# The attention sums as split float32r products in place of full fp32 products

## The chip, the core and the metric

The kernel runs on one core of a Trainium2 chip. The metric is device time in microseconds (us), the median of several executions; lower is better. Engines are named as in the profile: PE (TensorE matmuls), PEld (TensorE's loads of stationary weights, which overlap matmuls), DVE (VectorE), ACT (ScalarE), POOL (GpSimd) and SP (which issues the transfers).

## The reference

Input X has 4 batches of 512 rows with 512 features. For each batch the reference computes a modulated layer norm, an attention block whose "attention" is one vector per batch, and a feed-forward block:

```
Xn = layernorm(h); Q, K, V = split(Xn @ W_in + b_in)
K = rotary(K); V = rotary(V)                 # first 256 features
A = sum over rows of cos_sim(K) * cos_sim(V) # one vector of 512 per batch
A = 0.5 * A + 0.5
Y = (A * Q) @ W_out + b_out
...
out = x + gb * (relu(h2 @ W_up.T) @ W_down.T + h2 @ W_expert)
```

The change concerns the sum over rows that makes A, a vector with one number for each of the 512 features of a batch.

## The kernel before

Most products are done with operands split in a high and a low part of type float32r, `x = hi + lo`, and three matmuls (hi·hi, hi·lo, lo·hi); the helper `three` (lines 1032 to 1036) issues them, so that nearly all matmuls carry the lines 1034 to 1036. The tiles are 128 partitions wide; a batch has 4 row tiles (t) and 4 feature chunks (c or k).

The kernel has an order written out by hand for each engine, and semaphores between engines. For each batch b, `attention(b)` on PE does: the K and V tile of rows 0 (`kv_tile`), the output projection of the batch before (`out_rows_of(b - 1)`, which reads `g_hi` and `g_lo`), K and V of rows 1 to 3, four Q chunks (`feature_chunk`) with the transposes of the next batch between them, and last `a_sums(b)`. Then comes `kv_tile(b + 1, 0)`; behind batch 3 the feed-forward part begins with the logits (lines 1161 and 1162).

`acc`, 128 partitions by 768, gathers on DVE the weighted products of K and V over the four row tiles (`kv_sum`). After the last of them `a_pairs` (lines 734 to 737) folds the rotary part into `pair`, and `a_sums` adds over the 128 partitions: four full fp32 matmuls with 128x128 weights out of `pair` and `acc` and a one-column operand out of `half` (0.5 or 1). They write 4 columns of PSUM bank 6. That bank is also the one in which chunk 2 of the next batch's transposes stands until `t_split(b + 1, 2)` (line 688) on DVE has read it, and so `a_sums` waits for `afold` (the folding) and for the third `t_los` (that split).

Behind `a_sums`, DVE turns the sums into `a_col` and `ab_col` (`a_evac`, lines 741 and 744), ACT scales Q with them and rounds it to `g_hi` (lines 507 and 510), and DVE makes `g_lo` (`q_split`, line 748). `out_rows_of(b)` waits for these chunk by chunk.

POOL waits for the third `afold` of each batch (line 405) and then does, without another wait in batches 1 and 2, four `base` additions (line 356, both inputs in SBUF) and in batch 3 four `low_part` subtractions (line 330). In batch 0 it waits for `wlo_out` too, which DVE gives later.

`split_v` (lines 907 to 911) at the start of the kernel is a place where DVE does the same pair of operations as the change adds: a rounding copy of 128x512 and a subtraction of 128x512, all in SBUF.

Of the kernel before, what the change touches and what calls it, by code (L numbers as in the profile page):

```python
# [4 lines left out]
P = 128  # L5
B, S, D = 4, 512, 512
NT = S // P
NC = D // P
ROT = D // 4
# [4 lines left out]
IDENTITY_WEIGHT = 0.5  # L14
# [17 lines left out]
SUM_BANK = 6  # L32
# [3 lines left out]
def build(nc, X, cols, ident, rot, w, wmod, brow, out):  # L36
    f32 = mybir.dt.float32
    f32r = mybir.dt.float32r
    ALU = mybir.AluOpType
# [11 lines left out]
    with ctx:  # L51
        def sb(name, shape, dt=f32):
            return ctx.enter_context(nc.sbuf_tensor(name, shape, dt))

        def sem(name):
            return ctx.enter_context(nc.semaphore(name))
# [10 lines left out]
        g_hi = sb("g_hi", [P, NC, S], f32r)  # L67
        g_lo = sb("g_lo", [P, NC, S], f32r)
# [13 lines left out]
        acc = sb("acc", [P, D + 2 * ROT])  # L82
# [3 lines left out]
        gate_abs = hb[0:B, 1, 2:4]  # L86
        col = sb("col", [P, COLS])
        idn = sb("idn", [P, P])
        half = sb("half", [P, 2])
        xnm = sb("xnm", [P, NT])  # L90
        fold = cross[:].rearrange("p (i r) -> p i r", i=2)
        pair = sb("pair", [P, 2, ROT])
        ones = pair[0:1, 0, :]
        expo = sb("expo", [P, NT])
        sc = sb("sc", [P, NC * B])
        sc_t = sb("sc_t", [P, 3, NC * B])
# [19 lines left out]
        a_col = sb("a_col", [P, NC])  # L116
# [7 lines left out]
        tsum = sb("tsum", [P, NT])  # L124
# [3 lines left out]
        ps = ctx.enter_context(nc.psum_tensor("ps", [P, 8, 512], f32))  # L128
# [14 lines left out]
        cst = sem("cst")  # L143
# [16 lines left out]
        lg_ps2 = sem("lg_ps2")  # L160
        bc_ps = sem("bc_ps")
        afold = sem("afold")
        xst_s, xmv_s, xve_s, xrs_s = (sem(n) for n in ("xst_s", "xmv_s", "xve_s", "xrs_s"))
        xnm_s = sem("xnm_s")
        xn_s = sem("xn_s")
# [12 lines left out]
        a_ps, a_sb, ab_sb = sem("a_ps"), sem("a_sb"), sem("ab_sb")  # L178
# [134 lines left out]
        def _(pool):  # L313
# [3 lines left out]
            def rstd_x(g):  # L317
                pool.wait_ge(xve_s, g + 1)
                power(xrs[:], xve[:], NT, xrs_s)
# [94 lines left out]
                else:  # L414
                    low_part(5, whi, (3,) * NC, wlo_expert)

            pool.wait_ge(cst, 4)
            rstd_x(0)
            rstd_h(0, 0, 2)
            rstd_h(0, 2, 2)  # L420
# [185 lines left out]
        def _(dve):  # L606
            v = nc.vector
# [13 lines left out]
            def x_stats(g):  # L621
                dve.wait_ge(x_in, g * 16 + 16)
                for t in range(NT):
                    v.bn_stats(xst[:, t, :], xs[:, tok(g, t)]).then_inc(xst_s, 1)

            def x_aggr(g):
                for t in range(NT):
                    dve.wait_ge(xst_s, g * NT + t + 1)
                    v.bn_aggr(xmv[:, t, :], xst[:, t, :]).then_inc(xmv_s, 1)
                dve.wait_ge(xmv_s, g * NT + NT)  # L630
                v.tensor_scalar(xve[:], xmv[:, :, 1], EPS, None, ALU.add).then_inc(xve_s, 1)
# [97 lines left out]
            def a_pairs(b):  # L729


                dve.wait_ge(kacc, b * NT + NT)
                blocks = acc[:].rearrange("p (g i r) -> p g i r", g=3, i=2)
                v.tensor_tensor(fold, blocks[:, 0:3:2, 0, :], blocks[:, 0:3:2, 1, :], ALU.add).then_inc(afold, 1)
                dve.wait_ge(afold, b * 3 + 1)
                v.tensor_tensor(pair[:, 0, :], fold[:, 0, :], fold[:, 1, :], ALU.add).then_inc(afold, 1)
                v.tensor_tensor(pair[:, 1, :], fold[:, 0, :], fold[:, 1, :], ALU.subtract).then_inc(afold, 1)

            def a_evac(b):
                dve.wait_ge(a_ps, b + 1)  # L740
                v.tensor_scalar(a_col[:], ps[:, SUM_BANK, 0:NC], 1.0 - IDENTITY_WEIGHT, IDENTITY_WEIGHT,
                                ALU.mult, ALU.add).then_inc(a_sb, 1)
                dve.wait_ge(a_sb, b + 1)
                v.tensor_tensor(ab_col[:], a_col[:], col[:, COL_BQ:COL_BQ + NC], ALU.mult).then_inc(ab_sb, 1)

            def q_split(b, c):
                dve.wait_ge(q_his, b * NC + c + 1)
                v.tensor_tensor(g_lo[:, c, :], ps[:, Q_BANKS[c], :], g_hi[:, c, :].bitcast(f32),  # L748
                                ALU.subtract).then_inc(q_los, 1)
# [17 lines left out]
            def finish_rows(b):  # L767
                o_evac(b, 0)
                o_evac(b, 1)
                x2_out(b, 0)  # L770
                o_evac(b, 2)
                x2_out(b, 1)
                o_evac(b, 3)

            def attention(b):
                if b > 0:
                    a_evac(b - 1)
                    for c in range(NC):
                        q_split(b - 1, c)
                if b == 0:  # L780
                    x_stats(1)
                    x_aggr(1)
                    dve.wait_ge(const_in, N_CONST)
                    dve.wait_ge(row_out, 32)
                kv_rows(b, 0)
                if b == 0:
                    x_shift(1)
                kv_products(b, 0)
                if b > 0:
                    finish_rows(b - 1)  # L790
                    if b + 2 < B:
                        x_mean(b + 2)
                kv_sum(b, 0)
                if 0 < b < B - 1:
                    h_row(b + 1, 0)
                    h_row(b + 1, 1)
                    h_stats(b + 1, 0)
                    h_stats(b + 1, 1)
                    h_aggr(b + 1, 0, 2)
                elif b == B - 1:  # L800
                    for t in range(NT):
                        x2_rows(B, t)
                    h_aggr(B, 0, NT)
                kv_rows(b, 1)
                if b > 0 and b + 2 < B:
                    x_var(b + 2)
                kv_products(b, 1)
                if 0 < b < B - 1:
                    h_shift(b + 1, 0, 2)
                    h_row(b + 1, 2)  # L810
                    h_row(b + 1, 3)
                    h_stats(b + 1, 2)
                    h_stats(b + 1, 3)
                elif b == 0:
                    h_row(1, 0)
                    h_row(1, 1)
                    h_stats(1, 0)
                    h_stats(1, 1)
                    h_aggr(1, 0, 2)
                else:  # L820
                    h_shift(B, 0, NT)
                kv_sum(b, 1)
                kv_rows(b, 2)
                if 0 < b < B - 1:
                    h_aggr(b + 1, 2, 2)
                elif b == 0:
                    h_shift(1, 0, 2)
                    h_row(1, 2)
                    h_row(1, 3)
                    h_stats(1, 2)  # L830
                    h_stats(1, 3)
                    h_aggr(1, 2, 2)
                    x_mean(2)
                kv_products(b, 2)
                if b < B - 1:
                    h_shift(b + 1, 2, 2)
                if b + 2 < B and b > 0:
                    x_shift(b + 2)
                kv_sum(b, 2)
                kv_rows(b, 3)  # L840
                kv_products(b, 3)
                t_split(b + 1, 0)
                t_split(b + 1, 1)
                kv_sum(b, 3)
                a_pairs(b)
                if b == 0:
                    x_var(2)
                t_split(b + 1, 2)
                t_split(b + 1, 3)
                if b == 0:  # L850
                    x_shift(2)
                    for k in range(NC):
                        split_lo_out(k)

            v.memset(half[:, 0:1], 1.0).then_inc(cst, 1)
            v.memset(half[:, 1:2], 0.5).then_inc(cst, 1)
            v.memset(ones, 1.0).then_inc(cst, 1)
            v.memset(expo[:], -0.5).then_inc(cst, 1)
            dve.wait_ge(c_exp, 1)
            v.tensor_scalar(sc_t[:, 1, :], sc_t[:, 0, :], 1.0, None, ALU.add).then_inc(c_steps, 1)  # L860
            dve.wait_ge(c_steps, 1)
# [130 lines left out]
            def ffn(b):  # L992
# [23 lines left out]
                else:  # L1016
                    for i in range(len(LAST_PARTS)):
                        d_evac_last(i)

            a_evac(B - 1)  # L1020
            for c in range(NC):
                q_split(B - 1, c)
# [6 lines left out]
        def _(pe):  # L1029
            mm = nc.tensor.matmul  # L1030
# [54 lines left out]

            def a_sums(b):

                pe.wait_ge(afold, b * 3 + 3)
                pe.wait_ge(t_los, (b + 1) * NC + 3)
                a = ps[:, SUM_BANK, :]  # L1090
                mm(a[:, 0:1], pair[:, 0, :], half[:, 1:2], start=True, stop=True)
                mm(a[:, 1:2], pair[:, 1, :], half[:, 1:2], start=True, stop=True)
                mm(a[:, 2:3], acc[:, 2 * P:3 * P], half[:, 0:1], start=True, stop=True)
                mm(a[:, 3:4], acc[:, 3 * P:4 * P], half[:, 0:1], start=True, stop=True).then_inc(a_ps, 1)

            def out_rows_of(b):
                for t in range(NT):
# [161 lines left out]
```

## Time and profile before

| what | us |
|---|---|
| median of 3 executions (389.91 to 392.1) | 390.7 |
| the profiled execution: its own time | 388.38 |
| the profiled execution: span from first to last instruction | 386.6 |
| PE busy | 365.2 |
| DVE busy | 254.0 |
| ACT busy | 167.3 |
| POOL busy | 112.4 |

The span is shorter than the execution's own time by 1.8 us, which lie ahead of the first and behind the last instruction. The busy time of PE counts matmuls that overlap in the pipeline and is no measure of how well it is used.

### The profile page before, as it was taken

The page shows a single profiled execution, that of the slowest core. Times are in us where ns is not written, and L with a number is a line of the kernel's source. Part 1 is how long each engine was busy: PE and PEld are TensorE (multiplying, and loading weights), DVE is VectorE, ACT ScalarE, POOL GpSimd, SP SyncE. Part 2 cuts the span into 40 slices and gives each one's busy share as a digit, 9 for nine tenths or more (in the row PEclk, how much of TensorE's full clock was granted, in tenths as well). Part 3 has the DMA queues.
Part 4 walks back from the last instruction along what each step waited for, and adds up shares of the span by engine and source line. Part 5 has one row for each costly group of instructions (what it writes and reads, how often), then busy time and mean ns, then how long its engine had stood idle before and what let it go on. Part 6 is the DMA issues. An engine that isn't in the chain of part 4 may idle for free.

```text
span 386.6 us, 4661 instructions
## 1 busy us (share of the span) xinstructions
PE 365.2 (94%) x1664; PEld 286.1 (74%) x1664; DVE 254.0 (66%) x519; ACT 167.3 (43%) x293; POOL 112.4 (29%) x112
## 2 busy tenths in 40 slices
PE   4897998799989999999999999989999999999996
PEld 0156886687867778888788878868788878887885
DVE  0679799569978679886887556746560755084354
ACT  1337386685336830366215772147113612551210
POOL 0115683247842518425162151910001001000000
PEclk9997999899999999999999999999999999999999
DMA  7997972041001000000000003000200110011002
GB/s 226 384 376 253 362 255 89 0 137 27 2 20 63 0 0 2 27 2 2 0 29 0 0 2 108 28 2 27 81 2 0 54 57 0 0 57 54 2 0 109
DMA packets 10950, 27.42 MB, mean 71 GB/s; under 512 B 1184, under 2 KB 1568, under 8 KB 9776
## 3 DMA queue, kind: packets, MB, share of 16 engines
q1 hardware_dynamic: 10928, 27.13, 19.9%
q8 instruction: 13, 0.21, 0.2%
q14 instruction: 9, 0.07, 0.1%
HBM read 22.90 MB, written 4.23 MB: 70 GB/s over the span
## 4 chain that ended last, share of the span: by engine, by line
PE 72%; DVE 9%; ACT 5%; DMA 4%; issue 4%; POOL 4%; SPq 1%; POOLq 0%; DVEq 0%; ACTq 0%
PE ps L1034 21%; PE ps L1036 20%; PE ps L1035 20%; PE ps L1058 3%; PE ps L1041 3%; DMA xs<-in_wmod 2%; DMA xs<-in_X 2%; ACT sqj L448 1%; PE ps L1161 1%; PE ps L1162 1%; PE ps L1049 1%; DVE hb L662 1%; DVE ps L695 1%; POOL xs L350 1%; DVE acc L726 1%
## 5 line engine op out<-in xcount | busy, mean ns | idle before, releaser
L1034 PE MATMUL ps<-w_hi,t_hi 128*128 128x512 f32 x192 | 75.9, 396 | 1.3 <-DVE prod L707 1.3
L1035 PE MATMUL ps<-w_lo,t_hi 128*128 128x512 f32 x192 | 75.2, 392 | 0.0
L1036 PE MATMUL ps<-w_hi,t_lo 128*128 128x512 f32 x192 | 75.2, 392 | 0.0
L1034 PE MATMUL ps<-w_hi,g_hi 128*128 128x512 f32 (+1 forms) x132 | 51.5, 390 | 0.5 <-DVE g_lo L748 0.5
L1034 PE MATMUL ps<-t_hi,w_hi 128*128 128x512 f32 x128 | 51.8, 405 | 0.0
L1036 PE MATMUL ps<-w_hi,g_lo 128*128 128x512 f32 (+1 forms) x132 | 50.6, 383 | 0.0
L1035 PE MATMUL ps<-w_lo,g_hi 128*128 128x512 f32 (+1 forms) x132 | 50.6, 383 | 0.0
L1036 PE MATMUL ps<-t_hi,w_lo 128*128 128x512 f32 x128 | 50.5, 394 | 0.0
L1035 PE MATMUL ps<-t_lo,w_hi 128*128 128x512 f32 x128 | 50.5, 394 | 0.0
L688 DVE TENSOR_TENSOR t_lo<-ps,t_hi 128x512 fp32r<-128x512 f32 x32 | 21.8, 687 | 36.2 <-ACT t_hi L499 36.0
L1034 PEld LDWEIGHTS ps<-w_hi,t_hi 128*128 128x128 f32 x192 | 36.5, 190 | 9.2 <-issue 1.7
L1036 PEld LDWEIGHTS ps<-w_hi,t_lo 128*128 128x128 f32 x192 | 36.4, 190 | 7.7
L1035 PEld LDWEIGHTS ps<-w_lo,t_hi 128*128 128x128 f32 x192 | 36.5, 190 | 7.5
L324 POOL TENSOR_TENSOR hrs<-hve,expo 128x2 f32<-128x2 f32 (+1 forms) x12 | 10.7, 892 | 86.7 <-DVE hve L679 78.3
L448 ACT ACTIVATE sqj<-ps 128x512 bf16<-128x512 f32 x16 | 9.6, 597 | 56.7 <-DVE ps L695 43.4
L1034 PEld LDWEIGHTS ps<-w_hi,g_hi 128*128 128x128 f32 x132 | 24.8, 188 | 6.7 <-DVE g_lo L748 2.2
L1036 PEld LDWEIGHTS ps<-w_hi,g_lo 128*128 128x128 f32 x132 | 24.8, 188 | 4.9
L1036 PEld LDWEIGHTS ps<-t_hi,w_lo 128*128 128x128 f32 x128 | 24.4, 191 | 5.4
L1034 PEld LDWEIGHTS ps<-t_hi,w_hi 128*128 128x128 f32 x128 | 24.5, 191 | 5.2
L1035 PEld LDWEIGHTS ps<-w_lo,g_hi 128*128 128x128 f32 x132 | 24.8, 188 | 4.6
L1035 PEld LDWEIGHTS ps<-t_lo,w_hi 128*128 128x128 f32 x128 | 24.5, 191 | 4.9
L1058 PE MATMUL ps<-idn,z 128*128 128x128 f32 x128 | 18.6, 286 | 9.6 <-ACT z L485 4.9
(130 smaller groups left out, 601.0 us busy)
## 6 DMA issues: line engine op xcount, KB each, us to landing
xs<-in_X SPq DMA_DIRECT2D x4, 1024.0 KB, 7.2
stage<-in_w SPq DMA_DIRECT2D x4, 1024.0 KB, 6.9
out<-xs SPq DMA_DIRECT2D x15, 256.0 KB, 2.0
xs<-in_wmod SPq DMA_DIRECT2D x3, 1024.0 KB, 10.6
xs<-in_wmod SPq DMA_DIRECT2D x8, 256.0 KB, 7.0
stage<-in_w SPq DMA_DIRECT2D x8, 256.0 KB, 9.5
gate_bc<-mod_rows SPq DMA_DIRECT2D x8, 256.0 KB, 6.9
gate_bc<-in_wmod SPq DMA_DIRECT2D x1, 1024.0 KB, 12.6
```

The costliest lines, as they stand in the source:

```text
L324: nc.gpsimd.tensor_tensor(hrs[:, t0:t0 + n], hve[:, t0:t0 + n], expo[:, 0:n], ALU.pow).then_inc(hrs_s, n)
L350: nc.gpsimd.tensor_tensor(xs[:, tok(b, t)], xs[:, tok(b, t)], h, ALU.add).then_inc(x2_pool, 1)
L448: nc.scalar.activation(sqj[:], src, ACT.Square, accum_out=nsq[:, t % 2, i:i + 1]).then_inc(nsq_s, 1)
L662: v.tensor_tensor(h, h, sa_bc[:], ALU.add).then_inc(h1_s, 1)
L688: v.tensor_tensor(t_lo[:, g % 2, c, :], ps[:, T_BANKS[c % 2], :], t_hi[:, g % 2, c, :].bitcast(f32), ALU.subtract).then_inc(t_los, 1)
L695: v.tensor_tensor(ps[:, k_bank, :], ps[:, k_bank, :], bkv_bc[:, 0, :], ALU.add).then_inc(kb_s, 1)
L726: v.scalar_tensor_tensor(acc[:], prod[:], wgt[:, t % 2:t % 2 + 1], acc[:], ALU.mult, ALU.add).then_inc(kacc, 1)
L1034: mm(dst, l_hi, r_hi, start=start, stop=False)
L1035: mm(dst, l_hi, r_lo, start=False, stop=False)
L1036: return mm(dst, l_lo, r_hi, start=False, stop=stop)
L1041: last = mm(ps[0:B, bank, :], sc[:, k * B:(k + 1) * B], src[:, k * D:(k + 1) * D], start=(k == 0), stop=(k == NC - 1))
L1058: last = nc.tensor.transpose(ps[:, T_BANKS[c % 2], t * P:(t + 1) * P], z[:, t, c * P:(c + 1) * P], idn[:])
```

## The change

The folded sums go back into the first 256 columns of `acc` rather than into `pair`. A new function `a_split` on DVE rounds the 512 columns of `acc` to float32r in chunk 0 of `g_hi` and puts the remainder in chunk 0 of `g_lo`; both chunks are free at that place, between the output projection of the batch before and the Q chunks of this batch. `a_sums` then waits for `asplit` and issues eight float32r matmuls (a high and a low one for each of 4 chunks) with both columns of `half`; each chunk has two result columns, one with weight 1 and one with 0.5, and `a_evac` picks one of them in two instructions instead of one. At the start `half` is made by a copy, since it is float32r now.

```diff
+        half = sb("half", [P, 2], f32r)
+        sums_hi = g_hi[:, 0, :]
+        sums_lo = g_lo[:, 0, :]
...
-            pool.wait_ge(cst, 4)
+            pool.wait_ge(cst, 5)
...
-                v.tensor_tensor(pair[:, 0, :], fold[:, 0, :], fold[:, 1, :], ALU.add).then_inc(afold, 1)
-                v.tensor_tensor(pair[:, 1, :], fold[:, 0, :], fold[:, 1, :], ALU.subtract).then_inc(afold, 1)
+                v.tensor_tensor(acc[:, 0:ROT], fold[:, 0, :], fold[:, 1, :], ALU.add).then_inc(afold, 1)
+                v.tensor_tensor(acc[:, ROT:2 * ROT], fold[:, 0, :], fold[:, 1, :], ALU.subtract).then_inc(afold, 1)
+
+            def a_split(b):
+
+                dve.wait_ge(afold, b * 3 + 3)
+                v.tensor_copy(sums_hi, acc[:, 0:D]).then_inc(asplit, 1)
+                dve.wait_ge(asplit, b * 2 + 1)
+                v.tensor_tensor(sums_lo, acc[:, 0:D], sums_hi.bitcast(f32), ALU.subtract).then_inc(asplit, 1)
 
             def a_evac(b):
                 dve.wait_ge(a_ps, b + 1)
-                v.tensor_scalar(a_col[:], ps[:, SUM_BANK, 0:NC], 1.0 - IDENTITY_WEIGHT, IDENTITY_WEIGHT,
+                v.tensor_scalar(a_col[:, 0:2], ps[:, SUM_BANK, 1:4:2], 1.0 - IDENTITY_WEIGHT, IDENTITY_WEIGHT,
                                 ALU.mult, ALU.add).then_inc(a_sb, 1)
-                dve.wait_ge(a_sb, b + 1)
+                v.tensor_scalar(a_col[:, 2:4], ps[:, SUM_BANK, 4:8:2], 1.0 - IDENTITY_WEIGHT, IDENTITY_WEIGHT,
+                                ALU.mult, ALU.add).then_inc(a_sb, 1)
+                dve.wait_ge(a_sb, b * 2 + 2)
...
                 a_pairs(b)
+                a_split(b)
                 if b == 0:
                     x_var(2)
                 t_split(b + 1, 2)
...
+            dve.wait_ge(cst, 2)
+            v.tensor_copy(half[:], tsum[:, 0:2]).then_inc(cst, 1)
...
             def a_sums(b):
 
-                pe.wait_ge(afold, b * 3 + 3)
+                pe.wait_ge(asplit, b * 2 + 2)
                 pe.wait_ge(t_los, (b + 1) * NC + 3)
                 a = ps[:, SUM_BANK, :]
-                mm(a[:, 0:1], pair[:, 0, :], half[:, 1:2], start=True, stop=True)
-                mm(a[:, 1:2], pair[:, 1, :], half[:, 1:2], start=True, stop=True)
-                mm(a[:, 2:3], acc[:, 2 * P:3 * P], half[:, 0:1], start=True, stop=True)
-                mm(a[:, 3:4], acc[:, 3 * P:4 * P], half[:, 0:1], start=True, stop=True).then_inc(a_ps, 1)
+                for j in range(NC):
+                    mm(a[:, 2 * j:2 * j + 2], sums_hi[:, j * P:(j + 1) * P], half[:], start=True, stop=False)
+                    done = mm(a[:, 2 * j:2 * j + 2], sums_lo[:, j * P:(j + 1) * P], half[:], start=False, stop=True)
+                done.then_inc(a_ps, 1)
```

On DVE, at the end of batch 1 and in the order in which the engine takes them, the kernel before has these instructions (`t_lo` x2 are `t_split` of chunks 2 and 3 of the next batch):

```order
L726 SCALAR_TENSOR_TENSOR acc<-prod,wgt,acc 128x768
L734 TENSOR_TENSOR cross<-acc 128x256
L736 TENSOR_TENSOR pair<-cross 128x128
L737 TENSOR_TENSOR pair<-cross 128x128
L688 TENSOR_TENSOR t_lo<-ps,t_hi 128x512 x2
L741 TENSOR_SCALAR a_col<-ps 128x4
L744 TENSOR_TENSOR ab_col<-a_col,col 128x4
```

The changed kernel has at the same place of DVE (its line numbers are some higher: `t_split` is L691, `a_split` L745 and L747):

```order
L729 SCALAR_TENSOR_TENSOR acc<-prod,wgt,acc 128x768
L737 TENSOR_TENSOR cross<-acc 128x256
L739 TENSOR_TENSOR acc<-cross 128x128
L740 TENSOR_TENSOR acc<-cross 128x128
L745 CAST g_hi<-acc 128x512
L747 TENSOR_TENSOR g_lo<-acc,g_hi 128x512
L691 TENSOR_TENSOR t_lo<-ps,t_hi 128x512 x2
L751 TENSOR_SCALAR a_col<-ps 128x2
L753 TENSOR_SCALAR a_col<-ps 128x2
L756 TENSOR_TENSOR ab_col<-a_col,col 128x4
```

Two instructions of 128x512 stand between the folding and the two splits of the transposes now, and `a_col` is made in two.

## Rows read from the trace of the kernel before

**Rows 1.** The page: busy time by engine, and the chain that ended last by engine.
```profile
PE 365.2 (94%) x1664; PEld 286.1 (74%) x1664; DVE 254.0 (66%) x519; ACT 167.3 (43%) x293; POOL 112.4 (29%) x112
...
PE 72%; DVE 9%; ACT 5%; DMA 4%; issue 4%; POOL 4%; SPq 1%; POOLq 0%; DVEq 0%; ACTq 0%
```

**Rows 2.** PE's waits, smallest groups: total us, times, longest.
```profile
PE ps L1058 <- issue: 1.6, 1, 1.6
...
PE ps L1034 <- DVE g_lo L748: 0.5, 2, 0.3
```

**Rows 3.** PEld's timeline at the end of batch 1: start us, us, instruction.
```profile
129.83 0.41 PEld L1091 LDWEIGHTS ps<-half,pair 128*128 128x128 f32 x2
...
130.83 0.19 PEld L1034 LDWEIGHTS ps<-w_hi,t_hi 128*128 128x128 f32 x1
130.94 0.19 PEld L1035 LDWEIGHTS ps<-w_lo,t_hi 128*128 128x128 f32 x1
```

**Rows 4.** DVE's timeline at the end of batch 1.
```profile
127.70 0.42 DVE L734 TENSOR_TENSOR cross<-acc 128x256 f32<-128x256 f32 x1
128.16 0.29 DVE L736 TENSOR_TENSOR pair<-cross 128x128 f32<-128x128 f32 x1
128.37 0.28 DVE L737 TENSOR_TENSOR pair<-cross 128x128 f32<-128x128 f32 x1
128.57 1.28 DVE L688 TENSOR_TENSOR t_lo<-ps,t_hi 128x512 fp32r<-128x512 f32 x2
...
131.23 1.30 DVE L744 TENSOR_TENSOR ab_col<-a_col,col 128x4 f32<-128x4 f32 x1
```

**Rows 5.** POOL's timeline behind the folding of batches 0, 1 and 3.
```profile
82.26 10.11 POOL L356 TENSOR_TENSOR hb<-hb,bo_bc 128x512 f32<-128x512 f32 x8 [4.85 <-DVE w_lo L618]
...
128.73 5.02 POOL L356 TENSOR_TENSOR hb<-hb,bo_bc 128x512 f32<-128x512 f32 x4 [3.97 <-DVE pair L737]
...
222.10 5.03 POOL L330 TENSOR_TENSOR w_lo<-stage,w_hi 128x512 fp32r<-128x512 f32 x4 [7.68 <-DVE pair L737]
```

**Rows 6.** DVE's timeline, split_v of chunks 1 and 3 of a weight.
```profile
33.02 0.89 DVE L909 CAST w_hi<-stage 128x512 fp32r<-128x512 f32 x1
33.94 1.64 DVE L911 TENSOR_TENSOR w_lo<-stage,w_hi 128x512 fp32r<-128x512 f32 x1
...
38.77 0.42 DVE L909 CAST w_hi<-stage 128x512 fp32r<-128x512 f32 x1
39.23 0.69 DVE L911 TENSOR_TENSOR w_lo<-stage,w_hi 128x512 fp32r<-128x512 f32 x1
```

**Rows 7.** POOL's timeline beside split_v of chunk 1.
```profile
31.92 1.71 POOL L330 TENSOR_TENSOR w_lo<-stage,w_hi 128x512 fp32r<-128x512 f32 x1 [0.51 <-ACT w_hi L454]
...
33.71 1.32 POOL L330 TENSOR_TENSOR w_lo<-stage,w_hi 128x512 fp32r<-128x512 f32 x1
```

**Rows 8.** DVE's last folding instruction of batches 2 and 3.
```profile
175.12 0.29 DVE L737 TENSOR_TENSOR pair<-cross 128x128 f32<-128x128 f32 x1
...
221.73 0.28 DVE L737 TENSOR_TENSOR pair<-cross 128x128 f32<-128x128 f32 x1
```

**Rows 9.** PEld's first load of a_sums in batches 2 and 3.
```profile
176.59 0.41 PEld L1091 LDWEIGHTS ps<-half,pair 128*128 128x128 f32 x2
...
223.19 0.41 PEld L1091 LDWEIGHTS ps<-half,pair 128*128 128x128 f32 x2
```

**Rows 10.** DVE's timeline at the end of batch 0; in brackets idle time and releaser.
```profile
77.58 0.69 DVE L688 TENSOR_TENSOR t_lo<-ps,t_hi 128x512 fp32r<-128x512 f32 x1 [1.27 <-ACT t_hi L499]
...
82.13 0.16 DVE L744 TENSOR_TENSOR ab_col<-a_col,col 128x4 f32<-128x4 f32 x1
```

**Rows 11.** PE's timeline in the output projection of batch 1, around its fourth chunk.
```profile
138.20 0.39 PE L1036 MATMUL ps<-w_hi,g_lo 128*128 128x512 f32 x1
...
138.94 0.39 PE L1035 MATMUL ps<-w_lo,g_hi 128*128 128x512 f32 x1
```

**Rows 12.** PE's groups by line: busy us, mean ns of one, idle before.
```profile
L1049 PE MATMUL ps<-sc,gate_bc 128*128 128x4 f32 x32 | 3.7, 253 | 0.0
```

More of the change, by code:

```diff
@@ L88, in build @@
         idn = sb("idn", [P, P])
-        half = sb("half", [P, 2])
+        half = sb("half", [P, 2], f32r)
         xnm = sb("xnm", [P, NT])
         fold = cross[:].rearrange("p (i r) -> p i r", i=2)
-        pair = sb("pair", [P, 2, ROT])
-        ones = pair[0:1, 0, :]
+        pair = sb("pair", [1, ROT])
+        ones = pair[0:1, :]
+        sums_hi = g_hi[:, 0, :]
+        sums_lo = g_lo[:, 0, :]
         expo = sb("expo", [P, NT])
@@ L162, in build @@
         afold = sem("afold")
+        asplit = sem("asplit")
         xst_s, xmv_s, xve_s, xrs_s = (sem(n) for n in ("xst_s", "xmv_s", "xve_s", "xrs_s"))
@@ L853, in attention @@
                         split_lo_out(k)
-            v.memset(half[:, 0:1], 1.0).then_inc(cst, 1)
-            v.memset(half[:, 1:2], 0.5).then_inc(cst, 1)
+            v.memset(tsum[:, 0:1], 1.0).then_inc(cst, 1)
+            v.memset(tsum[:, 1:2], 0.5).then_inc(cst, 1)
             v.memset(ones, 1.0).then_inc(cst, 1)
             v.memset(expo[:], -0.5).then_inc(cst, 1)
+            dve.wait_ge(cst, 2)
+            v.tensor_copy(half[:], tsum[:, 0:2]).then_inc(cst, 1)
             dve.wait_ge(c_exp, 1)
```

## The prediction

> **What bounds the kernel now.** I read the page first: PE is busy 94% of the span and holds 72% of the chain that ended last [rows 1]. So what counts is whether PE issues without a break. The list of PE's waits comes next: behind the first 80 us it waits only in small pieces, among them 0.5 us for `g_lo` in the output projection of batch 0 and 1.6 us once in the feed-forward part [rows 2]. Any time by which PE is held or freed near `a_sums` therefore passes to the end, unless a later wait takes it up. That 1.6 us wait takes nothing up: it stands behind activations that follow from PE's own U chunks, and moves with them.
>
> Then the place itself, at the end of batch 1. PEld starts the loads for the sums at 129.83 and those of the next K tile at 130.83 [rows 3]. The third `t_los`, for which `a_sums` waits, comes from the first of the two `t_split` at 128.57; at 0.69 for one (the duration of such a subtraction in rows 6) it ends near 129.26 [rows 4, 6]. So PE's slack there is 129.83 − 129.26 = 0.57 us.
>
> **The products.** Before, four full fp32 products make eight loads and eight matmul records. Their loads take 130.83 − 129.83 = 1.00 us: the first waits 0.22 for the running matmul, the other seven follow at 0.11 [rows 3]. After, eight float32r products make eight loads. The first float32r load behind them was followed by the next after 130.94 − 130.83 = 0.11 us [rows 3], the same pace. Two products that add into the same few columns back to back have a row too: 32 records of 128x4 took 3.7 us, 0.115 each, in groups of four that accumulate [rows 12]. So I put the products at no change. Bounds: if they fell to nothing, 1.00 − 0.22 = 0.78 us a batch would be freed (3.1 us in all); if each cost the 0.25 that one record lasts instead of 0.115 [rows 12], 8 × 0.135 = 1.1 us a batch would be added (4.3 us).
>
> **The two DVE instructions without POOL.** The rounding copy takes 0.42 and the subtraction 0.69 where nothing disturbs them [rows 6]. A dependent DVE instruction starts 0.04 after the one before has ended (127.70 + 0.42 = 128.12, next at 128.16), and an independent one some 0.08 before that end (128.37 + 0.28 = 128.65, next at 128.57) [rows 4]. In batch 1 the folding ends at 128.37 + 0.28 = 128.65, the copy runs 128.69 to 129.11, the subtraction 129.15 to 129.84, and the `t_split` that PE needs runs from 129.76 to 130.45, 1.2 us later than now. With 0.05 to reach PE, an estimate near DVE's own 0.04, the loads start at 130.50, 0.67 late. Of this 0.11 comes back, since after a wait the second load follows 0.11 and not 0.22 behind the first. That is 0.56 us in batch 1, and the same sum gives 0.56 in batch 2 (folding ends 175.41, loads at 176.59) and in batch 3 (222.01 and 223.19) [rows 8, 9]. In batch 0 DVE sits idle 1.27 us for ACT ahead of that `t_split` [rows 10]; 0.42 + 0.69 + 2 × 0.04 = 1.19 fits into it, so the cost is nothing; without that cover it would be the same 0.56.
>
> **The two DVE instructions with POOL.** In batches 1 and 3, POOL's four instructions start at 128.73 and 222.10, 0.08 and 0.09 after the folding has ended [rows 4, 5, 8], just where `a_split` now begins; batch 2 has the same order of work. They have SBUF inputs and last 5.02 / 4 = 1.25 each. What such neighbours do to this very pair of DVE instructions is shown by `split_v`: beside POOL the copy took 0.89 instead of 0.42 and the subtraction 1.64 instead of 0.69 [rows 6]. The copy ended 0.28 after POOL's instruction had ended (31.92 + 1.71 = 33.63, copy 33.91). POOL's next ended at 33.71 + 1.32 = 35.03, some 1.12 after that copy, and the subtraction 0.55 later, at 35.58 [rows 6, 7]. So they took turns. Nearer by is `ab_col`, 128x4, which took 1.30 beside `base` [rows 4] and 0.16 where POOL was idle [rows 10]. The `t_split`, with one input in PSUM, kept its 1.28 for two while POOL ran from 128.73 on [rows 4, 5], so only the two new ones are hit. The Trainium skill, SBUF — State Buffer, Who interferes with whom, speaks against the change here: a VectorE instruction with two SBUF inputs contends with a GpSimd one that reads SBUF, the pair of ports goes whole to whoever starts first, and the other stands still until the end. By that rule alone the copy, if it starts first, goes free and the subtraction waits out one POOL instruction, which is the sum below; the rows above bear it out.
>
> In batch 1 the copy is due at 128.69 and POOL at 128.73, so I let DVE win: copy to 129.11, POOL's first then to 129.11 + 1.12 = 130.23, the subtraction to 130.78, `t_split` to 131.39, PE's loads at 131.44: 1.61 late, 1.50 net of the 0.11. Batch 2: folding ends 175.41, loads at 178.20 instead of 176.59: 1.50. Batch 3: 222.01, 224.80 instead of 223.19: 1.50. Sum 4.5 us.
>
> **What comes back.** Behind the sums, `ab_col` is stuck behind POOL now: 131.23 to 132.53. After the change POOL runs 0.4 to 1 us later and `ab_col` comes some 1.8 us later, behind a second `a_col` (0.1 us); it then ends about 0.9 to 1.1 us later than now, while PE is 1.5 later. In batch 1 PE waits shortly for the last `g_lo`: two matmuls on it stands at 138.94 instead of 138.20 + 2 × 0.23 = 138.66 (0.23 is the step left of the 1.00 above when seven of 0.11 go off), so 0.28 is lost there [rows 11] and comes back. Batch 2 has the same order of work, and I take the same. So −0.6 us in all. Batch 3 has the logits and two expert tiles ahead of its projection, and none.
>
> **The rest.** In batch 0 `ab_col` would move by 0.07 to 82.20, and POOL's eight additions start at 82.26 [rows 5, 10]. I let `ab_col` win and take nothing, since ACT normalises four tiles of batch 2 there before it can use it; if it lost, it would wait 1.25 and delay Q's chain, and PE which already waits for it [rows 2], by about 1.0. The small copy for `half` and POOL's fifth `cst` lie under the first loads, tens of us before anybody needs them: nothing, and with no cover 0.2. `base` and `low_part` end about 1 us later: `base` is read a whole batch later, and `wlo_expert` by an expert tile that moves 1.5 us itself.
>
> **Sum.** 4.5 − 0.6 = +3.9 us on the profiled execution, 388.38 to 392.3. That execution lies 2.3 under the median of the three; the step added to the median 390.7 gives 394.6, 1.0% slower.
>
> **The rivals.**
> *POOL first.* The order at the folding's end hangs on 0.04 us. If POOL takes the ports first, the copy waits until 128.73 + 1.25 + 0.28 = 130.26, POOL's second instruction runs to 131.38, the subtraction to 131.93 and the `t_split` to 132.54; PE is 2.76 late, 2.65 net. Three batches less 0.6: +7.4, 398.1. For it: `ab_col` loses every time POOL already runs. Against: DVE's own semaphore has reached it in 0.04, POOL in 0.08 [rows 4, 5].
> *No turns taken.* If the new pair is not held, the cost is 3 × 0.56 − 0.6 = +1.1, 391.8, which is no change to a measurement. Against: rows 6 and 7 show the same pair held.
> *The products get cheaper, and the kernel faster.* The place is PE between 129.83 and 130.83; the price is at most 0.78 us a batch. Over four batches it decides from 3.9 / 4 = 1.0 us a batch on if DVE is held, which is more than there is, and from 1.1 / 4 = 0.28 on if it isn't: at best 1.1 − 3.1 = −2.0, 388.7. With DVE held it gives at best +0.8, 391.5. Against: float32r loads pace at 0.11 [rows 3]. The Trainium skill, TensorE: Matmul & The Clock Gate, Weight-path perf modes, has fast weight loads for types other than FP32, but no win at four bytes an element; taken without that limit, a fourfold load would by estimate give some 2.4 of these 3.1 us. The trace's own 0.11 for float32r decides here.
>
> **How the numbers follow.** I give the forecast 0.60 (0.1 of it with batch 0's `ab_col` losing, 395.6), POOL first 0.13, no turns 0.17, cheaper products 0.06 (half of it on the faster side), and 0.04 to costlier products (up to +4.3 more). A measurement of this kernel tells about 0.5%, 2 us, from no change. Slower: 0.60 + 0.13 + 0.04 = 0.77; within 0.5%: 0.17 + 0.03 = 0.20; faster: 0.03. The range goes from the case without turns, 391.8 with a little noise, to POOL first, 398.1: 391.5 to 398.4. That leaves out the cheapest and the dearest products, under 2 in 10. The likeliest case alone spans 393.6 to 395.9.
>
> **What would show it.** In the trace after: the new subtraction near 1.6 us in batches 1 to 3 and 0.69 in batch 0, the copy 0.42; PE with a wait of about 1.5 us ahead of the first product in batches 1 to 3 and none in batch 0; eight products with loads 0.11 apart; no wait for `g_lo` in batches 1 and 2. I would be wrong if the subtraction shows 0.69 there, if the copy shows 1.5, or if the eight products together differ from 1 us by more than some tenths.

## The result, and the profile after

The changed kernel takes 397.77 us (median of 4, 397.38 to 398.31), the kernel before 390.49 (median of 4); the ratio is 1.0187 with a 95% interval of 1.0146 to 1.0227, 7.3 us slower. The time lies in the predicted range (391.5 to 398.4) and on the side that was forecast, but the step is nearly twice the predicted one (3.9). Ratios, here and below, leave out executions that lie over 1.5% above the fastest of their kernel: one of the kernel before, at 527.93, and two of six of the kernel with the split and full fp32 products, 398.28 and 398.36.

The page of the changed kernel, as in [rows 1] (`a_split` is L745 and L747 now, `t_split` L691, the sums L1107 and L1108, the helper for three products L1049 to L1051, `base` L359):

```profile
span 395.6 us, 4674 instructions
...
PE 369.9 (93%) x1664; PEld 288.6 (73%) x1664; DVE 258.8 (65%) x532; ACT 167.3 (42%) x293; POOL 114.5 (29%) x112
```

PE has the same number of records, 1664: the four full fp32 products left two records each, the eight float32r products leave one each. PE's waits have a group that was not there, the first of these two; the second, for `g_lo` in batch 0, is as in [rows 2]:

```profile
PE ps L1107 <- DVE t_lo L691: 4.1, 3, 1.4
...
PE ps L1049 <- DVE g_lo L760: 0.5, 2, 0.3
```

Three waits of 1.4 us stand ahead of the first product of the sums, and they are for the split of the transposes that DVE now reaches later. DVE's timeline at the end of batch 1, beside [rows 4]:

```profile
131.91 0.43 DVE L745 CAST g_hi<-acc 128x512 fp32r<-128x512 f32 x1
132.37 1.67 DVE L747 TENSOR_TENSOR g_lo<-acc,g_hi 128x512 fp32r<-128x512 f32 x1
133.96 1.28 DVE L691 TENSOR_TENSOR t_lo<-ps,t_hi 128x512 fp32r<-128x512 f32 x2
...
136.11 0.31 DVE L756 TENSOR_TENSOR ab_col<-a_col,col 128x4 f32<-128x4 f32 x1
```

POOL's timeline at the same place, beside [rows 5]:

```profile
131.96 5.67 POOL L359 TENSOR_TENSOR hb<-hb,bo_bc 128x512 f32<-128x512 f32 x4 [3.97 <-DVE acc L740]
```

The copy starts 0.05 ahead of POOL and takes 0.43, as long as where nothing disturbs it. The subtraction takes 1.67, 0.98 more than its 0.69; 1.67 is what the forecast has for waiting out POOL's first instruction. POOL's four take 5.67 instead of 5.02. In batch 0, where POOL has nothing to do at that moment, the subtraction is as short as predicted:

```profile
79.46 0.69 DVE L747 TENSOR_TENSOR g_lo<-acc,g_hi 128x512 fp32r<-128x512 f32 x1
```

So far this is the forecast. What is new stands in PE's timeline behind the wait of batch 1:

```profile
133.03 0.39 PE L1051 MATMUL ps<-t_hi,w_lo 128*128 128x512 f32 x1
134.79 0.24 PE L1107 MATMUL ps<-half,g_hi 128*128 128x2 f32 x1 [1.36 <-DVE t_lo L691]
...
135.56 0.25 PE L1108 MATMUL ps<-half,g_lo 128*128 128x2 f32 x1
135.67 0.53 PE L1049 MATMUL ps<-w_hi,t_hi 128*128 128x512 f32 x1
136.00 0.63 PE L1050 MATMUL ps<-w_lo,t_hi 128*128 128x512 f32 x1
136.42 0.63 PE L1051 MATMUL ps<-w_hi,t_lo 128*128 128x512 f32 x1
...
138.98 0.58 PE L1051 MATMUL ps<-w_hi,t_lo 128*128 128x512 f32 x1
139.41 0.40 PE L1049 MATMUL ps<-w_hi,t_hi 128*128 128x512 f32 x1
139.64 0.40 PE L1050 MATMUL ps<-w_lo,t_hi 128*128 128x512 f32 x1
```

The sums start 134.79 − 133.03 = 1.76 behind the last matmul of Q, where 0.23 is the step: 1.53 late. The eight products take 135.67 − 134.79 = 0.88, 0.11 each; from the first of them to the next matmul it was 0.81 before, and is 0.81 in batch 0 now, where PE does not wait. So the work behind the sums is 1.60 late, for 1.50 predicted. But from 136.00 to 139.41 eight matmuls step by 0.43 instead of 0.23: TensorE's clock is at its lower level of the two (1.2 GHz instead of 2.4) over these 3.4 us, and that costs 8 × 0.2 = 1.6 us. The windows by batch of the same execution (columns: window, its length, busy time and count of PE, PEld, DVE, ACT and POOL, then the granted clock, the DMA share and GB/s):

```profile
132.00:141.00 9.00, 7.64 (x31) 5.99 (x30) 5.66 (x10) 7.31 (x12) 5.63 (x4) 0.81 0.00 0
...
180.00:190.00 10.00, 8.64 (x44) 7.00 (x43) 6.64 (x13) 6.09 (x11) 5.70 (x4) 1.00 0.01 2
...
228.00:240.00 12.00, 10.64 (x53) 7.96 (x51) 7.97 (x16) 9.21 (x13) 5.70 (x4) 1.00 0.01 1
```

In this execution the clock fell in batch 1 (0.81) and not in batches 2 and 3, though all three waited 1.36 us.

The span grew by 395.6 − 386.6 = 9.0, more than the medians did. At the first product of the sums of batch 0 the changed kernel already stands at 82.36, the one before at 79.17: 3.2 us lost ahead of anything that the change moves but the copy for `half`. In the chain of work of the first 50 us (the kernel before, then the changed one) the first weights land 0.6 later and the eight matmuls behind them take 1.7 longer, with a granted clock of 0.84 from 20 to 30 us where the kernel before has 1.00:

```profile
24.98 3.54 PE ps L1041 x8
...
25.58 5.24 PE ps L1056 x8
```

The other 0.9 are lost behind 45 us; behind PE's long wait for ACT there the granted clock was 0.59 (73 to 79 us), and 0.72 in the kernel before (70 to 76 us). Whether the slower start belongs to the change is the first open question; the other is whether the clock fell because PE stood still.

### The profile page after: what moved, and what is told of

It reads as the page before. It is cut to its first block, busy times and chain, and to the rows that moved or that the text cites. A ratio compares the mean times of both kernels' runs of the same rounds, so it can differ in the third digit from the quotient of the medians.

```text
span 395.6 us, 4674 instructions
## 1 busy us (share of the span) xinstructions
PE 369.9 (93%) x1664; PEld 288.6 (73%) x1664; DVE 258.8 (65%) x532; ACT 167.3 (42%) x293; POOL 114.5 (29%) x112
## 4 chain that ended last, share of the span: by engine, by line
PE 60%; DVE 13%; ACT 7%; issue 7%; POOL 7%; DMA 4%; SPq 1%; POOLq 0%; DVEq 0%; ACTq 0%
PE ps L1049 17%; PE ps L1050 17%; PE ps L1051 17%; PE ps L1056 3%; DMA xs<-in_wmod 2%; PE ps L1073 2%; DMA xs<-in_X 2%; DVE acc L729 2%; ACT sqj L451 2%; POOL hb L351 2%; POOL xs L353 2%; ACT ps L500 1%; POOL hb L368 1%; DVE g_lo L747 1%; ACT t_hi L502 1%
## 5 line engine op out<-in xcount | busy, mean ns | idle before, releaser
L1049 PE MATMUL ps<-w_hi,t_hi 128*128 128x512 f32 x192 | 76.7, 400 | 1.3 <-DVE prod L710 1.3
L1050 PE MATMUL ps<-w_lo,t_hi 128*128 128x512 f32 x192 | 76.2, 397 | 0.0
L1051 PE MATMUL ps<-w_hi,t_lo 128*128 128x512 f32 x192 | 76.1, 397 | 0.0
L1049 PE MATMUL ps<-t_hi,w_hi 128*128 128x512 f32 x128 | 51.8, 405 | 0.0
L1049 PE MATMUL ps<-w_hi,g_hi 128*128 128x512 f32 (+1 forms) x132 | 51.3, 389 | 0.5 <-DVE g_lo L760 0.5
L1051 PE MATMUL ps<-w_hi,g_lo 128*128 128x512 f32 (+1 forms) x132 | 50.6, 383 | 0.0
L1051 PE MATMUL ps<-t_hi,w_lo 128*128 128x512 f32 x128 | 50.6, 395 | 0.0
L691 DVE TENSOR_TENSOR t_lo<-ps,t_hi 128x512 fp32r<-128x512 f32 x32 | 21.7, 686 | 35.5 <-ACT t_hi L502 35.3
L1049 PEld LDWEIGHTS ps<-w_hi,t_hi 128*128 128x128 f32 x192 | 37.1, 193 | 9.5 <-issue 1.7
L1051 PEld LDWEIGHTS ps<-w_hi,t_lo 128*128 128x128 f32 x192 | 36.9, 192 | 8.0
L1049 PEld LDWEIGHTS ps<-w_hi,g_hi 128*128 128x128 f32 x132 | 24.8, 188 | 5.9 <-DVE g_lo L760 1.3
L1051 PEld LDWEIGHTS ps<-w_hi,g_lo 128*128 128x128 f32 x132 | 24.8, 188 | 4.9
L1049 PEld LDWEIGHTS ps<-t_hi,w_hi 128*128 128x128 f32 x128 | 24.6, 192 | 5.2
L1051 PEld LDWEIGHTS ps<-t_hi,w_lo 128*128 128x128 f32 x128 | 24.5, 191 | 5.3
```

What stands on the lines that cost most here:

```text
L691: v.tensor_tensor(t_lo[:, g % 2, c, :], ps[:, T_BANKS[c % 2], :], t_hi[:, g % 2, c, :].bitcast(f32), ALU.subtract).then_inc(t_los, 1)
L1049: mm(dst, l_hi, r_hi, start=start, stop=False)
L1050: mm(dst, l_hi, r_lo, start=False, stop=False)
L1051: return mm(dst, l_lo, r_hi, start=False, stop=stop)
```

## The experiments

Each ratio is to the kernel before, run beside it on the same chip. Its median was 390.15 (27 executions, all but one from 388.03 to 393.07) beside the kernels with only the start, POOL behind the split, no low part, and full fp32 products, and 390.44 (17 executions, 387.65 to 392.71) beside the other four.

**Only the start of the change** (the kernel before with one copy more).

```diff
+        half_r = sb("half_r", [P, 2], f32r)
...
-            pool.wait_ge(cst, 4)
+            pool.wait_ge(cst, 5)
...
+            dve.wait_ge(cst, 2)
+            v.tensor_copy(half_r[:], half[:]).then_inc(cst, 1)
```

> The kernel before with only the start of the change: one small copy to float32r more on DVE, and POOL waits for it. Theory (the start differs from execution to execution by itself): 390.5, no change. Rival (the slower start belongs to these instructions): 2 to 3 us slower, about 393.

Measured: 390.14, ratio 0.9995 (0.9964 to 1.0026). Its 12 executions go from 388.19 to 392.85, as those of the kernel before do. So the copy and POOL's wait for it do not cost 3 us: the interval leaves room for 1. The start differs from execution to execution, and the profile of before [rows 1] is from a good one: 388.38 where the median is 390.5.

**POOL behind the split.**

```diff
-                pool.wait_ge(afold, b * 3 + 3)
+                pool.wait_ge(asplit, b * 2 + 2)
```

> POOL waits for the split of the sums rather than for the folding, so that it can't run beside the two new DVE instructions; all else is as in the changed kernel. Theory (POOL holds the subtraction, and the wait of 1.6 us that follows lets TensorE's clock fall in batch 1): the subtraction takes 0.69 in all batches, PE waits about 0.6 ahead of the sums of batches 1 to 3 instead of 1.6, the granted clock is 1.00 from 80 us on, and the time is about 1.1 us over the kernel before, 391.6 (changed kernel 397.8). Rival (the start of the kernel, slower by about 3 us in the profile after, belongs to the change): about 394.5.

Measured: 391.45, ratio 1.0016 (0.9987 to 1.0045). One line of order takes nearly all of the loss away. The subtraction (the group of L747 with its shortest, median and longest), PE's wait, and the window of batch 1:

```profile
L747 DVE TENSOR_TENSOR g_lo<-acc,g_hi x4: 691/692/693, 78.9 to 225.8; 128x512 fp32r<-128x512 f32 x4
...
PE ps L1107 <- DVE t_lo L691: 1.2, 3, 0.4
...
128.00:142.00 14.00, 12.99 (x65) 10.43 (x64) 9.40 (x19) 11.30 (x19) 5.02 (x4) 1.00 0.00 0
```

It takes 0.69 in all four batches, PE waits 0.4 and not 1.4 (0.6 was expected; the sums start 0.55 late), POOL's four are back at 5.02, and the granted clock is 1.00 in every window from 79 to 240 us. The time is 1.3 over the kernel before by the medians, 1.1 was expected.

**Without the low part** (the sums leave out the low part: no subtraction, four products).

```diff
-                dve.wait_ge(asplit, b * 2 + 1)
-                v.tensor_tensor(sums_lo, acc[:, 0:D], sums_hi.bitcast(f32), ALU.subtract).then_inc(asplit, 1)
...
-                pe.wait_ge(asplit, b * 2 + 2)
+                pe.wait_ge(asplit, b + 1)
...
-                    mm(a[:, 2 * j:2 * j + 2], sums_hi[:, j * P:(j + 1) * P], half[:], start=True, stop=False)
-                    done = mm(a[:, 2 * j:2 * j + 2], sums_lo[:, j * P:(j + 1) * P], half[:], start=False, stop=True)
+                    done = mm(a[:, 2 * j:2 * j + 2], sums_hi[:, j * P:(j + 1) * P], half[:], start=True, stop=True)
```

> The sums go without their low part: only the rounding copy is left of the two new DVE instructions, and only four float32r products with two columns. Theory: the copy (0.42) fits into the slack of 0.57 that PE has in batches 1 to 3, no wait appears ahead of the sums, and the time is that of the kernel before less 4 x 0.45 for four loads fewer, about 388.7 (within 387.7 to 390.5). Rival (slower start): about 391.5. Rival (float32r products cost more than full fp32): above 391.

Measured: 388.1, ratio 0.9937 (0.9899 to 0.9975), 2.05 us faster than the kernel before; 1.8 was expected. No wait stands ahead of the sums. PEld's timeline at the end of batch 1, beside [rows 3]:

```profile
128.97 0.64 PEld L1105 LDWEIGHTS ps<-half,g_hi 128*128 128x128 f32 x4
129.53 0.19 PEld L1047 LDWEIGHTS ps<-w_hi,t_hi 128*128 128x128 f32 x1
129.64 0.19 PEld L1048 LDWEIGHTS ps<-w_lo,t_hi 128*128 128x128 f32 x1
```

Four loads take 129.53 − 128.97 = 0.56, where eight took 1.00: 0.11 for each one less. The copy alone makes no wait; what the products cost is the count of their loads, and that the change leaves at eight. That 2.05 comes so near to 1.8 is in part luck: in the trace the 0.45 of batch 0 go for the most part into longer waits for `g_lo` (from the sums of batch 0 to those of batch 1 it takes 50.90, before 50.88), while in batches 1 and 2 more than 0.45 comes back (0.84 and 0.69).

**The split, with the products in full fp32.**

```diff
-                    mm(a[:, 2 * j:2 * j + 2], sums_hi[:, j * P:(j + 1) * P], half[:], start=True, stop=False)
-                    done = mm(a[:, 2 * j:2 * j + 2], sums_lo[:, j * P:(j + 1) * P], half[:], start=False, stop=True)
+                    done = mm(a[:, 2 * j:2 * j + 2], acc[:, j * P:(j + 1) * P], half[:].bitcast(f32), start=True, stop=True)
```

> The split of the sums on DVE stays and is waited for, but the products are four in full fp32 out of the unsplit sums, as before the change. Theory (the loss is DVE's two instructions and not the form of the products): 397.8 as the changed kernel, with the same waits of 1.6 ahead of the sums. Rival (the products cost): the time lies between the kernel before and the changed kernel, by as much as the products cost.

Measured: 397.58, median of 6, as the changed kernel; the ratio is 1.0112 (1.0049 to 1.0176) over the four shorter executions. The waits ahead of the sums are again 4.1 us in three. Its fastest execution tells most: 392.28 at a mean granted clock of 0.987. The kernel before has 388.03 to 388.30 in its executions at 0.985 to 0.987. With the clock at the same height the split costs 4.0 to 4.3 us; what other executions have more (395.67 at 0.978, 397.03 at 0.974, 398.13 at 0.970) goes with the clock, that of the start included, which varies in the kernel before too (393.07 at 0.972). The windows of its profile, at 397.03, have the clock below 1.00 behind two of the three waits:

```profile
128.00:142.00 14.00, 12.63 (x54) 10.31 (x55) 9.74 (x16) 9.85 (x16) 5.67 (x4) 0.88 0.00 0
...
176.00:190.00 14.00, 12.65 (x57) 10.04 (x56) 9.39 (x17) 8.45 (x14) 5.68 (x4) 0.88 0.01 1
...
225.00:240.00 15.00, 13.62 (x69) 10.43 (x68) 10.27 (x18) 10.78 (x16) 5.70 (x4) 1.00 0.01 2
```

**The changed kernel again.**

> The changed kernel itself once more, for the spread of its times beside the others of this call. From the trace: about 4 us of waits in batches 1 to 3, and on top of it 1.6 us for each of these batches in which the granted clock falls behind the wait. Theory (the clock falls in most batches, not in all): times between 392 and 399, median about 397.6.

Measured: 396.99, 393.67 to 398.23, ratio 1.0152 (1.0104 to 1.0201). Two of six executions, 393.67 and 394.18, have a mean clock of 0.982; the four others, 396.3 to 398.23, have 0.978 to 0.969. The profiled one (397.68) has the clock below 1.00 behind the waits of batches 1 and 2 (0.91 in 128 to 146 us, 0.91 in 176 to 196) and 1.00 behind that of batch 3.

**The wait filled** (six matmuls of which nobody reads the result, in a PSUM bank that is free there).

```diff
+                if b > 0:
+                    pe.wait_ge(kv_sb, b * NT + NT)
+                    pe.wait_ge(kprod, b * NT + NT)
+                    pe.wait_ge(t_los, (b + 1) * NC + 1)
+                    for _ in range(6):
+                        mm(ps[:, 0, :], t_hi[:, (b + 1) % 2, 0, 0:P], w_hi[:, WO, 0, :], start=True, stop=True)
                 pe.wait_ge(asplit, b * 2 + 2)
```

> As the changed kernel, but PE issues six more matmuls of 128x512, whose result nobody reads, ahead of the sums of batches 1 to 3: 6 x 0.23 = 1.4 us of work in the place of the wait of 1.6. The sums start at the same moment. Theory (the wait itself costs 4 us, and the rest is TensorE's clock that falls because PE stands still): granted clock 1.00 from 100 to 240 us, time 390.2 + 4.0 = 394.2. Rival (the rest is something else): 397.6 as the changed kernel, or up to 1 us more.

Measured: 394.1, ratio 1.0106 (1.0068 to 1.0144); five of six executions lie between 393.92 and 394.51, the sixth at 396.46. This kernel does more work than the changed one and is 2.9 us faster than it (396.99 beside it). PE's timeline and the window of batch 1:

```profile
131.29 0.39 PE L1051 MATMUL ps<-t_hi,w_lo 128*128 128x512 f32 x1
131.51 1.52 PE L1108 MATMUL ps<-w_hi,t_hi 128*128 128x512 f32 x6
133.03 0.24 PE L1113 MATMUL ps<-half,g_hi 128*128 128x2 f32 x1
...
133.92 0.47 PE L1049 MATMUL ps<-w_hi,t_hi 128*128 128x512 f32 x1
134.23 0.39 PE L1050 MATMUL ps<-w_lo,t_hi 128*128 128x512 f32 x1
```
```profile
128.00:146.00 18.00, 17.73 (x83) 14.62 (x84) 13.26 (x27) 11.57 (x20) 6.85 (x6) 1.00 0.00 0
```

The sums start 1.74 behind the last matmul of Q, as in the changed kernel (1.76), so the delay is the same; the matmuls behind them step by 0.23 at once. The granted clock is 1.00 in the windows of batches 2 and 3 too.

**The subtraction twice.**

```diff
-                dve.wait_ge(asplit, b * 2 + 1)
+                dve.wait_ge(asplit, b * 3 + 1)
...
+                dve.wait_ge(asplit, b * 3 + 2)
+                v.tensor_tensor(sums_lo, acc[:, 0:D], sums_hi.bitcast(f32), ALU.subtract).then_inc(asplit, 1)
...
-                pe.wait_ge(asplit, b * 2 + 2)
+                pe.wait_ge(asplit, b * 3 + 3)
```

> The subtraction of the split is done twice in each batch, so that DVE meets POOL once more. Theory (DVE and POOL take turns): each of the two subtractions takes about 1.67 in batches 1 to 3, PE waits 1.67 longer there, 5.0 us in all; with the wait at 3.1 us the granted clock falls behind it in all three batches (in the changed kernel in one to three of them), so about 397.6 + 5.0 + up to 1.7 = 402.6 to 404.3. Rival (no turns, the second one runs free): 397.6 + 3 x 0.7 = 399.7.

Measured: 407.81 (403.85 to 408.28), ratio 1.0426 (1.038 to 1.0473), more than either theory gave. DVE and then PE at the end of batch 1:

```profile
131.47 1.67 DVE L747 TENSOR_TENSOR g_lo<-acc,g_hi 128x512 fp32r<-128x512 f32 x1
133.17 1.64 DVE L749 TENSOR_TENSOR g_lo<-acc,g_hi 128x512 fp32r<-128x512 f32 x1
```
```profile
132.14 0.39 PE L1053 MATMUL ps<-t_hi,w_lo 128*128 128x512 f32 x1
135.56 0.34 PE L1109 MATMUL ps<-half,g_hi 128*128 128x2 f32 x1 [3.03 <-DVE t_lo L691]
...
137.26 0.77 PE L1051 MATMUL ps<-w_hi,t_hi 128*128 128x512 f32 x1
...
142.00 0.39 PE L1053 MATMUL ps<-w_hi,t_lo 128*128 128x512 f32 x1
```

The turns are as expected: 1.67 and 1.64, and a wait longer by 1.67 (3.03 for 1.36). The clock was under-sized: in batch 1 it is low already when the sums start, so that the eight products take 137.26 − 135.56 = 1.70 instead of 0.88, and the eleven matmuls behind them 4.74 instead of about 2.6. That is 2.9 us in this batch, not 1.6. In the profiled execution, at 406.03, the windows of all three batches (128 to 146, 176 to 196, 224 to 246 us) are below 1.00:

```profile
128.00:146.00 18.00, 14.36 (x57) 11.61 (x57) 11.45 (x19) 10.84 (x18) 6.11 (x4) 0.81 0.00 0
176.00:196.00 20.00, 16.97 (x79) 13.72 (x78) 14.84 (x27) 12.38 (x22) 7.23 (x6) 0.91 0.00 1
224.00:246.00 22.00, 18.97 (x89) 14.35 (x88) 13.65 (x25) 14.91 (x22) 7.25 (x6) 0.92 0.00 1
```

In batches 2 and 3 the products still take 0.88 (batch 2 below), the clock falls behind them, and the cost is 1.6 each as in the changed kernel:

```profile
188.23 0.24 PE L1109 MATMUL ps<-half,g_hi 128*128 128x2 f32 x1 [3.03 <-DVE t_lo L691]
...
189.11 0.48 PE L1051 MATMUL ps<-w_hi,t_hi 128*128 128x512 f32 x1
```

So the three waits give 3 × 3.27 − 0.6 = 9.2 and the clock 2.9 + 1.6 + 1.6 = 6.1 in this execution. The step by the medians, 17.4, leaves 8.2 for the clock: four of the six executions, 407.7 to 408.28, have a lower mean clock (0.958) than the profiled one (0.962).

**The kernel before, POOL later.**

```diff
-                pool.wait_ge(afold, b * 3 + 3)
+                if b < B - 1:
+                    pool.wait_ge(ab_sb, b + 1)
+                else:
+                    pool.wait_ge(afold, b * 3 + 3)
```

> The kernel before, with POOL's additions of batches 0 to 2 waiting for ab_col rather than for the folding, so that ab_col is not held. Theory (the 0.28 us that PE waits for the last g_lo in batches 1 and 2 come from ab_col being held): ab_col takes 0.16 in batches 0 to 2, the waits for g_lo in batches 1 and 2 go, 390.15 - 0.6 = 389.6. Rival (PE waits there for ACT anyway): 390.15.

Measured: 389.7, ratio 0.9967 (0.9938 to 0.9996), 0.7 us faster; the interval just leaves out no change. The trace is a surer witness: from the sums of batch 1 to those of batch 2 it takes 46.43 instead of 46.76, and on to those of batch 3 46.28 instead of 46.61, 0.33 less each. `ab_col` takes 0.16 now in every batch, and in batch 1 the fourth chunk of the output projection comes at PE's own step (0.23 and 0.23, where [rows 11] had 0.74 for the two):

```profile
140.19 0.39 PE L1039 MATMUL ps<-w_hi,g_lo 128*128 128x512 f32 x1
140.42 0.39 PE L1037 MATMUL ps<-w_hi,g_hi 128*128 128x512 f32 x1
140.65 0.39 PE L1038 MATMUL ps<-w_lo,g_hi 128*128 128x512 f32 x1
```

It computes all of the reference and is the fastest full version here, by little.

## Why the prediction was right, and where its size came from

- **The products at no change: right.** Eight float32r loads at 0.11; 0.81 us from the first product to the next matmul in batch 0, before and after; with the products back in full fp32 and the split kept, the time stays at 397.6.
- **DVE alone, without POOL: right.** 0.43 and 0.69 in batch 0, hidden there, and `ab_col` of batch 0 (at 85.42) still ahead of POOL (at 85.48). With POOL kept away the sums are 0.55 late in batches 1 to 3, for 0.56 in the sum, and the kernel is 1.3 us over the one before; 1.1 was the sum of that rival, whose mechanism (no turns) was not what happened in the changed kernel.
- **DVE and POOL take turns, DVE first: right.** Copy 0.43, subtraction 1.67 where the steps give 1.67 (129.11 to 130.78). The rule of the Trainium skill, SBUF — State Buffer, Who interferes with whom, by which whoever starts first keeps the ports for its whole instruction, agrees with these rows. The work behind the sums is 1.60 late for 1.50, since the first load for them starts 1.71 late and not 1.61. That the measured time lies near the rival with POOL first (398.1) is chance: DVE was first in all three batches.
- **What comes back: right.** `ab_col` shrinks from 1.30 to 0.31, and in batch 1 PE goes through the output projection at its own step; the experiment with the kernel before shows its worth, 0.33 in each of batches 1 and 2 for the 0.28 of the prediction.
- **The sum: short by a term that is missing.** It took a wait of PE to cost its own length ("Any time by which PE is held or freed near `a_sums` therefore passes to the end"). The length comes out nearly as predicted: 1.53 and 0.07 for the restart is 1.6 a batch, 4.8 in three, 4.2 after the 0.6 that comes back, and 4.0 to 4.3 was measured where the clock stayed up. The other 3 us are the clock behind the wait, 1.6 us each time it falls, and by the medians it falls in about two of the three batches. The filled wait shows it: same delay, no standing still, 394.1. That 397.77 still lies in the range is luck, since the top of the range was set by the order of POOL and DVE and not by the clock.
- **The same without the start.** Counted from the first product of batch 0's sums to the end of the span, the traces take 386.6 − 79.17 = 307.43 (the kernel before), 392.3 − 80.63 = 311.67 (the wait filled), 395.6 − 82.36 = 313.24 (the changed kernel) and 395.9 − 81.07 = 314.83 (the changed kernel again). Over the kernel before that is 4.2, 5.8 and 7.4 us: 4.2 and no fall of the clock, one, and two, at 1.6 each. The first products, in this order:

```profile
79.17 0.28 PE L1091 MATMUL ps<-half,pair 128*128 128x1 f32 x2
...
80.63 0.17 PE L1113 MATMUL ps<-half,g_hi 128*128 128x2 f32 x1
...
82.36 0.17 PE L1107 MATMUL ps<-half,g_hi 128*128 128x2 f32 x1
...
81.07 0.17 PE L1107 MATMUL ps<-half,g_hi 128*128 128x2 f32 x1
```

- **A wait that would have warned, and one that would not.** The trace of the kernel before had such a price in it, ahead of the 80 us from which the prediction read the waits: behind a wait of 4.16 us six matmuls step by 0.43, from 71.73 to 74.29, 1.2 us lost. The 1.6 us wait of PE in the feed-forward part [rows 2] has none: in the windows that cover it, before and after, the clock is 1.00.

```profile
70.25 1.25 PE L1058 MATMUL ps<-idn,z 128*128 128x128 f32 x8 [4.16 <-ACT z L485]
...
71.73 0.63 PE L1035 MATMUL ps<-t_lo,w_hi 128*128 128x512 f32 x1
72.16 0.63 PE L1036 MATMUL ps<-t_hi,w_lo 128*128 128x512 f32 x1
```

What stays open: why the clock falls behind the same 1.36 us wait in one batch and not in the next, within one execution. The runs show which executions had it, not what decides it.

## What to carry to other kernels

When DVE work is put where another engine is released by the same semaphore, look at what that engine does next: each DVE subtraction with two SBUF inputs took 1.0 us longer beside a row of POOL instructions here (1.67 for 0.69), and moving POOL's wait by one step was worth 6 us of 7. A product with few columns costs the loads of its weights; trading four fp32 products for eight float32r ones leaves eight loads, and there was nothing to win. A wait on TensorE can have a second price in the matmuls that follow it: behind 1.4 us of standing still it was 1.6 us more in some batches here and nothing in others.

## What the runs showed of the hardware

- Six useless matmuls in the place of a wait made the kernel 2.9 us faster (394.1 for 396.99), because TensorE's clock stayed at its upper level.
- Waits of 0.4 us did not lower it in the one profile that has them (granted clock 1.00). Waits of 1.4 us ahead of the sums did in five of the nine batches of three profiles, at 1.6 us each time. Waits of 3.03 did in all three batches of one profile, at 2.9, 1.6 and 1.6 us.
- The order of DVE and POOL at one semaphore was the same in the three batches of the changed kernel: DVE's own instruction starts 0.04 to 0.05 ahead of POOL's (131.91 and 131.96 in batch 1) and takes 0.43. In [rows 6] and [rows 7], where a POOL instruction ran already, a copy of the same shape took 0.89.
